# Second attention: which engine scales which score pair by its reciprocal row sums

## The reference, cut to what matters

```python
q = (latents @ Wq).reshape(bsz, q_len, HEADS, HEAD_DIM).transpose(0, 2, 1, 3)
k = (kv @ Wk)...            # 8 key/value heads, kv = context (64 rows) and latents (256 rows)
q = rms_norm(q, q_norm_w)
k = rms_norm(k, k_norm_w)
scores = jnp.einsum('bhgqd,bhkd->bhgqk', qg, k) * scale
probs = jax.nn.softmax(scores.astype(jnp.float32), axis=-1).astype(q.dtype)
out = jnp.einsum('bhgqk,bhkd->bhgqd', probs, v)
return out @ Wo
```

## Time and profile before

| | us |
|---|---|
| median of 3 runs | 1514.88 |
| fastest and slowest of them | 1511.53 and 1515.43 |
| time of the profiled execution | 1515.12 |
| its span, first to last instruction | 1513.3 |

### The profile page before, as it was taken

How to read it: one execution, slowest core, us unless ns; L and a number is a source line. 1 busy time by engine, 2 the same in 40 slices (tenths; PEclk the granted TensorE clock), 3 DMA queues, 4 the chain that set the end, 5 groups by cost and what they waited for, 6 DMA issues and landing times. The chain is left out here.

```text
span 1513.3 us, 24457 instructions
## 1 busy us (share of the span) xinstructions
PE 1424.4 (94%) x8064; PEld 1210.9 (80%) x8064; DVE 1114.1 (74%) x2922; ACT 795.7 (53%) x2201; POOL 427.0 (28%) x512
## 2 busy tenths in 40 slices
PE   5999999999899998999999999999999999999889
PEld 4888888887778887788888888888788888887767
DVE  7888888888651535778778778787787787777765
ACT  5667666666320314565565565555555655555521
POOL 4733334442691831121111111111111211112120
PEclk9999999999999999999999999999999999999989
DMA  4111111110230310100101001001001001010001
GB/s 188 71 47 65 64 60 69 69 42 29 84 101 27 85 79 0 70 1 21 50 1 69 0 0 69 0 0 69 0 0 69 0 2 67 16 39 1 1 1 56
DMA packets 14934, 63.76 MB, mean 42 GB/s; under 512 B 1760, under 2 KB 1760, under 8 KB 10656
## 3 DMA queue, kind: packets, MB, share of 16 engines
q1 hardware_dynamic: 14880, 63.07, 11.8%
HBM read 60.97 MB, written 2.10 MB: 42 GB/s over the span
## 5 line engine op out<-in xcount | busy, mean ns | idle before, releaser
L1206 ACT ACTIVATE p<-psum,nb,rq 128x320 f32<-128x320 f32 x256 | 155.1, 613 | 162.4 <-DVE nb L989 162.4
L55 PE MATMUL psum<-w1q_hi,xnT_lo 128*128 128x512 f32 x256 | 107.6, 420 | 6.5 <-DVE pT_lo L954 6.5
L954 DVE TENSOR_TENSOR pT_lo<-psum,pT_hi 128x512 fp32r<-128x512 f32 x128 | 88.2, 690 | 33.1 <-ACT pT_hi L1129 31.4
L985 DVE TENSOR_REDUCE mx<-psum 128x2 f32<-128x640 f32 x128 | 105.1, 821 | 5.6
L434 ACT ACTIVATE p<-psum,nb 128x64 f32<-128x64 f32 x256 | 76.8, 313 | 50.9 <-DVE nb L344 50.8
L919 POOL TENSOR_TENSOR rk<-ssk,rms_eps 128x3 f32<-128x3 f32 x32 | 6.3, 196 | 344.7 <-DVE ssk L1026 344.7
L55 PE MATMUL psum<-w1o_hi,oT_lo 128*128 128x512 f32 x256 | 100.7, 393 | 0.0
L57 PE MATMUL psum<-w1q_hi,xnT_hi 128*128 128x512 f32 x256 | 100.7, 393 | 0.0
L56 PE MATMUL psum<-w1o_lo,oT_hi 128*128 128x512 f32 x256 | 100.5, 393 | 0.0
L57 PE MATMUL psum<-w1o_hi,oT_hi 128*128 128x512 f32 x256 | 100.1, 391 | 0.0
L56 PE MATMUL psum<-w1q_lo,xnT_hi 128*128 128x512 f32 x256 | 99.7, 389 | 0.0
(11 more groups left out here) (250 smaller groups left out, 4804.1 us busy)
## 6 DMA issues: line engine op xcount, KB each, us to landing
raw_q<-in_w0q SPq DMA_DIRECT2D x8, 1024.0 KB, 4.8
raw_o<-in_w0o SPq DMA_DIRECT2D x8, 1024.0 KB, 4.7
raw_q<-in_w1q SPq DMA_DIRECT2D x8, 1024.0 KB, 7.5
raw_o<-in_w1o SPq DMA_DIRECT2D x8, 1024.0 KB, 4.8
raw_kv<-in_w_gu SPq DMA_DIRECT2D x10, 512.0 KB, 3.6
raw_gu<-in_w_gu SPq DMA_DIRECT2D x10, 512.0 KB, 3.6
raw_kv<-in_w0kv SPq DMA_DIRECT2D x8, 515.0 KB, 3.3
raw_kv<-in_w1kv SPq DMA_DIRECT2D x8, 512.0 KB, 5.5
```

The costliest lines, as they stand in the source:

```text
L55: pe.matmul(out, w[1], m[0], start=start, stop=False)
L954: last = dve.tensor_tensor(k.pT[1][:, kt, 2 * hp:2 * hp + 2, :], bank.rearrange("p (h q) -> p h q", h=2), f(k.pT[0][:, kt, 2 * hp:2 * hp + ...
L985: dve.tensor_reduce(k.mx[:, stat(j)], s_pair(j), AX.X, ALU.max).then_inc(mx_ready, 1)
L1206: last = act.activation(k.p1[:, tile, h, :], s_pair(j)[:, h % 2, :], ACT.Exp, bias=k.nb[:, i:i + 1], scale=k.rq[:, i:i + 1], accum_out=k.r ...
```

## The change

Pair 0 is scaled by DVE instead of POOL, pairs 2 and 3 by POOL instead of DVE. DVE has pairs 0 and 1, POOL has pairs 2 and 3. The reciprocals stay on DVE for all four. PE's two semaphore waits follow: both the first transpose (hp 0) and transpose 3 (hp 1) now wait for one pair of DVE and one of POOL.

```diff
@@ -925,7 +925,8 @@
                     pool.tensor_tensor(k.rq[:, :], k.rq[:, :], k.minus_half[:, 0:8], ALU.pow).then_inc(rq_ready, 1)
-                    p_scale(n, 0)
+                    p_scale(n, 2)
+                    p_scale(n, 3)
@@ -993,7 +994,7 @@
                 dve.reciprocal(k.rinv[:, stat(j)], k.rs[:, stat(j)]).then_inc(rinv_ready, 1)
-                if j == 0:
+                if j >= 2:
                     return
                 dve.wait_ge(rinv_ready, 4 * n + j + 1)
@@ -1229,9 +1230,8 @@
                 if kt == 0:
-                    if hp == 0:
-                        pe.wait_ge(p_scaled_pool, n)
-                    pe.wait_ge(p_scaled, 3 * (n - 1) + 2 + hp)
+                    pe.wait_ge(p_scaled, 2 * (n - 1) + 1 + hp)
+                    pe.wait_ge(p_scaled_pool, 2 * (n - 1) + 1 + hp)
```

## The result

| kernel | median, us | runs | lowest to highest | ratio to before, 95% interval |
|---|---|---|---|---|
| before, measured beside the change | 1513.62 | 6 | 1511.53 to 1515.43 | |
| changed | 1519.93 | 6 | 1517.92 to 1521.14 | 1.0039 [1.0026, 1.0052] |
| changed, a second measurement (`r_after_again`) | 1519.38 | 8 | | 1.0028 [1.0017, 1.0039] |

The kernel became slower by 0.3 to 0.4%, some 4 to 6 us. I had forecast 1515.5 us and no change. The first median lies 0.1 us above the high end of the range, the second inside it; both lie near the price of rival 1, 1520.1, which had a chance of 0.12. By the first ratio the kernel is slower by over 0.3%, which had 0.12; by the second it is within 0.3%. That the range reaches so far at all is owed to rival 1, for whose sake its high end was stretched, and not to the step that failed.

What follows compares the result with a forecast made beforehand. PE was taken as the bound (97.69 of 100 us in attention 1). The terms 0 + 0 + 0 + 0.6 gave +0.6 us, so 1515.5 us from a median of 1514.88; range 1511.5 to 1519.8 us.

Steps and rivals of the forecast that it cites:

- rival 1: Boundary b = 0 to 1: DVE's second split gets in before POOL, PE 0.78 us late; 4.6 us slower, 1520.1; chance 0.12.
- What bounds the kernel, and the costs of the work: Attention 1: PE bounds; 21.8 us of DVE work go, 40.1 us of POOL work come, neither a gain or loss itself.
- Pair 0 on DVE: Between reciprocal and x_add 0: 0.68 us fits DVE's 0.66 us idle, cost 0; at b = 3 DVE's list shifts 0.3 us.
- Boundaries b = 2 to 3, 3 to 0 and 1 to 2: Pair 2 on POOL ends before PE's transposes: spare 0.19 us, 0.22 us, and more at the last; cost 0.
- Boundary b = 0 to 1, the collision: POOL's pair 2 meets a weight split: 1.78 us from split start to POOL's end at 1031.05; both splits 2.33 us.
- 0.18 us late ... swallowed: 0: Boundary b = 0 to 1: PE's transposes start 0.18 us late, hidden by ACT's later copy and PE's 0.35 us wait; cost 0.
- The brush with splits 2 and 3: At b = 0 to 1, POOL's pair 3 overlaps the next split by 0 to 0.1 us, 8 times; taken as 0.
- First unit: Behind unit 0: POOL's pair costs 0.6 to 1.1 us, but PE's 1.14 us wait before transpose 3 stays: 0 within 0.1.
- Last unit: Behind unit 31: no k and v matmuls cover POOL's pair 2, PE's transposes start 0.58 us late; cost +0.6 us.
- rival 3: Granted clock behind unit 31: a half-clock stretch comes or goes, 3 us either way, 1512.5 or 1518.5; chance 0.05.
- The sum: Whole kernel: nothing in the loop, 0.6 at the end, +0.6 us in all, giving 1515.5 us.
- What would show it: Signs in the profile after; the prediction is wrong if units come over 0.1 us closer or wider, or PE waits at b = 2 to 3.

Runs made afterwards that it cites:

- pair-3 variant: Kernel before with POOL scaling pair 3 instead of pair 0 in every unit: 1515.29 us; with splits w1o_lo 2 and 3 also moved, 1512.84 us.

## Why the prediction was right in part and wrong in part, step by step

- **What bounds the kernel, and the costs of the work: right.** DVE's busy time fell by 15 us (less than the 21.8 of the sum, mostly since a held split counts as busy) and POOL's rose by 43, and the time followed neither; POOL's pair is 1.254 us.
- **Pair 0 on DVE: right.** In the changed kernel the scaling runs at 1048.92 and x_add 0 follows without the 0.66 us of idle of the earlier trace rows. DVE's timeline:

```profile
1048.72 0.17 DVE L996 RECIPROCAL rinv<-rs 128x2 f32<-128x2 f32 x1 [0.40 <-ACT p L1207]
1048.92 0.68 DVE L1001 TENSOR_SCALAR p<-p,rinv 128x320 f32<-128x320 f32 x2
1049.55 0.75 DVE L972 SCALAR_TENSOR_TENSOR x<-psum,gate,x 128x512 f32<-128x512 f32 x1
```

- **Boundaries b = 2 to 3, 3 to 0 and 1 to 2: right, cost 0.** Their steps stand at 25.57, 27.61 and 27.22. The spare of 0.19 and 0.22 us was less than I wrote, since PE needs 0.24 us behind POOL's end and not 0.06 (below): by that it was about nought at b = 2 to 3, and it held.
- **Boundary b = 0 to 1, the collision: right.** POOL's scaling 1.62 us, the two splits 2.33 us, POOL's end at +1.86 after the reciprocal's start, as 1031.05 - 1029.19 = 1.86 had it. POOL got its turn between the splits, so the cause named in rival 1 didn't occur.
- **The same boundary, "0.18 us late ... swallowed: 0": wrong, and this is the step that failed**, by three sizes. First, PE's start behind POOL's end. I took 0.06 us from the earlier trace rows in attention 0; here it is 1031.40 - 1031.16 = 0.24. The instruction stream of PE in the trace shows what stands between. In attention 0 the wait for POOL is on the weight load itself. In the loop it is an instruction of its own on PE's sequencer, recorded from 1031.20 to 1031.25; behind it comes a second one, from 1031.31 to 1031.35, with the wait of L1239, and only then weight load and matmul at 1031.40. Behind the first and the last unit the wait for POOL is an instruction of its own too, but the only one before the weight load, and PE starts 0.10 (604.14 behind 604.04) and 0.11 us (1436.62 behind 1436.51) after POOL. So PE was 0.36 late instead of 0.18. Second, the spare on ACT. I put the end of transpose 0 at half of the group's 1.04 us and got 0.28 spare; a row of four such instructions is 0.63 to 0.66 long, and I should have read it there. In the changed kernel, where ACT waits for PE, its copy starts 1032.09 - 1031.40 = 0.69 us behind PE's start; before it was 1031.68 - 1030.93 = 0.75. So the spare was 0.06, and 0.36 - 0.06 is the 0.30 by which ACT is late; even the 0.18 of the forecast would have cost 0.12. Third, the wait before transpose 3. I called it a cover for PE's delay. It is the end of the chain PE, ACT, pT_lo, splits, pT_lo, PE, and covers only a delay that doesn't travel down that chain.
- **The chance of rival 1.** The prediction said that it decides "from 0.3 us more delay on, where ACT has no spare left". By its own numbers the point lay only 0.28 - 0.18 = 0.10 us away, and with the spare of 0.06 the forecast delay was past it already. The path of rival 1 came true at less than half its price, 0.27 x 7 = 1.9 us instead of 4.6, with another first cause.
- **The brush with splits 2 and 3: taken as 0, and right.** Their duration stands at 1.28 us, and after pT_lo nothing is added to the 0.3 (the table above).
- **First unit: nearly right** (-0.12 us at the first step; 0 within 0.1 was said). **Last unit: right.** PE started 0.62 us later, 0.58 was said, and kernels with equal time at half clock differ by 0.62 us from unit 31 on. But the sum took the drain by itself and left the clock to rival 3 with 0.05, while the stretches at half clock behind the last unit take 10 to 20 us from one execution to the next and move the end by 1 to 2 us.
- **The sum.** 1.9 - 0.24 for the loop and 0.6 for the drain make 2.3 us, where +0.6 was forecast. Three of the six profiles with the changed loop have 1.5 us more from the stretch at half clock; if that belongs to the change, which isn't shown, it adds 0.75 on average: 3.0 us. That lies in the second measurement's interval (2.6 to 5.9 us), and 2.3 lies just below it; the first one's (3.9 to 7.9 us) stays above 3.0 by 0.9 us, and I have no account for that part but the low median that before had in that session. At equal clock, where such a stretch should cancel for the most part, 2.7 to 3.8 us were measured. So 0.4 us or more beyond the 2.3 has no account; the clock is known to 0.001 only, and the medians of before differ by about 0.9 us for each 0.001.
- **What would show it.** Of the signs that the prediction named, these came: 64 instructions of L912, 1.6 us at b = 0, a PE wait for POOL of 0.2 us (seven times, 1.4 us in all), 0.35 falling to 0.2, a w1o_lo of 1.7 us, the idle time before x_add 0. At b = 3 the first of POOL's two scalings is drawn out too (the two take 2.83 us together from 1002.89). The sign that was to decide, units not more than 0.1 us wider, failed at one kind of boundary in four, and the mean step over all units, which I named as well, hides it: 0.27 us in every fourth is 0.07.

What stays open: what lowers the clock at units 29 to 30, why the all-DVE last unit shortens the end by 2 us and not 0.6 in its two profiles, and that its nine runs reach from 1515.1 to 1520.7 us. The chain from PE over ACT and DVE back to PE is read from the rows of two kernels; no run cut it at one link, as the changed kernel with splits 2 and 3 moved away would have.

## What to carry to other kernels

Work moved to an idle engine costs what its later end costs the next engine in the chain, so read the spare at every link, from the row of just the instructions that release it, and not as a share of a merged group. A wait seen further down a chain absorbs a delay only if what it waits for isn't itself delayed; ask what feeds it before calling it a cover. Where the work of two engines collides, look first for whether one part, here a weight split with time to spare, can stand elsewhere: that took away the whole cost at the boundary b = 0 to 1, and the same move on the other two splits made the kernel before and its pair-3 variant faster by 0.15%.

## What the runs showed of the hardware

- How long after POOL's end PE starts differs with what stands on its sequencer in between: 0.06 us where the wait is on the weight load itself (attention 0), 0.10 and 0.11 us with one wait instruction before it (first and last unit), 0.24 us with two (the boundary b = 0 to 1 in the loop).
- POOL and DVE take turns: started 0.16 us into a DVE split of 0.67 us, POOL's scaling took 1.62 us instead of 1.25, and the next split ended only 0.55 us behind it (2.33 us for the two, 1.29 alone). DVE had the next split ready behind the first, and POOL got in between all the same, seven times of seven. The Trainium skill (SBUF — State Buffer, SBUF: two separate sides) has the two share a port pair that is locked for a whole instruction; the rows agree, and add that the one that waits isn't passed over by back-to-back work of the other.
- Single stretches at 1.2 GHz came and went between executions of one and the same kernel. The one at units 29 to 30, 3.4 us long, cost 1.5 us, more than half of the 2.8 us by which that profile is the longer one.
